# Interleaved first matmul groups, context rounding and small loads moved, and a new bank for the last half tile

## What is computed

```python
query = jnp.einsum('bnc,dc->bnd', teacher_features, Wq) + bq
key = jnp.einsum('bnc,dc->bnd', teacher_features, Wk) + bk
energy = jnp.einsum('bnd,bmd->bnm', query, key)
attention = jax.nn.softmax(energy, axis=-1)
x_m = jnp.einsum('bln,bmn->blm', teacher_logits, attention)
...
x = x + jnp.tanh(g_xattn[0]) * _L0_xattn_ref(_layernorm(x, axis=-1), ctx_1024, L0_xattn_Wq, L0_xattn_bq, L0_xattn_Wk, L0_xattn_bk)
x = x + jnp.tanh(g_ffn[0]) * _L0_ffn_ref(_layernorm(x, axis=-1), L0_ffn_weight, L0_ffn_gamma, L0_ffn_beta, L0_ffn_ln_weight, L0_ffn_ln_bias)
```

## Time and profile before

| | us |
|---|---|
| median of three runs | 124.51 |
| lowest, highest | 123.63, 124.8 |
| the profiled execution's own time | 123.77 |
| its span, first to last instruction | 121.9 |

### The profile page before, as it was taken

How to read it: one execution, slowest core, us unless ns; L and a number is a source line. 1 busy time by engine, 2 the same in 40 slices (tenths; PEclk the granted TensorE clock), 3 DMA queues, 4 the chain that set the end, 5 groups by cost and what they waited for, 6 DMA issues and landing times.

```text
span 121.9 us, 1882 instructions
## 1 busy us (share of the span) xinstructions
PE 116.8 (96%) x564; PEld 94.7 (78%) x564; DVE 94.8 (78%) x188; ACT 87.3 (72%) x186; POOL 93.0 (76%) x106
## 2 busy tenths in 40 slices
PE   5989999999999999999999999999999999999990
PEld 4658788888887988878888888888898888888870
DVE  1169599897898996769956993799749948989972
ACT  2455999999999979476998795659987962246200
POOL 3007999918247998999995999994748999999960
PEclk9999999999999999999999999999999999999998
DMA  4988999915813220027671302557000012220045
GB/s 92 273 291 286 404 386 321 345 52 163 239 41 132 95 77 5 3 86 255 261 258 25 147 5 86 167 177 232 27 3 3 0 74 103 86 86 0 0 168 176
DMA packets 10649, 17.15 MB, mean 141 GB/s; under 512 B 1808, under 2 KB 2576, under 8 KB 10640
## 3 DMA queue, kind: packets, MB, share of 16 engines
q1 hardware_dynamic: 9504, 16.78, 40.5%
q10 hardware_dynamic: 1136, 0.27, 1.0%
HBM read 12.59 MB, written 4.19 MB: 138 GB/s over the span
## 4 chain that ended last, share of the span: by engine, by line
PE 88%; DVE 6%; issue 2%; ACT 1%; DVEq 0%; ACTq 0%
PE ps_y L390 37%; PE ps_ffn L403 18%; PE ps_score L350 8%; PE ps_turn L357 5%; PE ps_score L357 3%; PE ps_score L464 3%; PE ps_y L357 3%; PE ps_y L320 2%; PE ps_turn L320 2%; PE ps_ffn L320 2%; DVE zt_lo L734 2%; PE ps_ffn L329 1%; PE ps_turn L350 1%; PE ps_ffn L456 1%; DVE ps_ffn L811 1%
## 5 line engine op out<-in xcount | busy, mean ns | idle before, releaser
L896 POOL TENSOR_TENSOR xt_lo<-xt_raw,xt_hi 128x512 fp32r<-128x512 f32 x16 | 21.1, 1319 | 5.8 <-ACT xt_hi L535 2.9
L390 PE MATMUL ps_y<-pt_hi,xt_hi 128*128 128x512 f32 x64 | 18.1, 404 | 0.0
L390 PE MATMUL ps_y<-pt_hi,xt_lo 128*128 128x512 f32 x64 | 17.5, 395 | 0.0
L390 PE MATMUL ps_y<-pt_lo,xt_hi 128*128 128x512 f32 x64 | 17.5, 395 | 0.0
L403 PE MATMUL ps_ffn<-w_sign,zt_hi 128*128 128x512 f32 x60 | 17.2, 408 | 0.0
L403 PE MATMUL ps_ffn<-w_sign,zt_lo 128*128 128x512 f32 x60 | 16.5, 396 | 0.0
L523 ACT ACTIVATE prob<-ps_score,neg_max 128x512 f32<-128x512 f32 x14 | 9.6, 687 | 9.5 <-DVE neg_max L676 9.5
L390 PEld LDWEIGHTS ps_y<-pt_lo,xt_hi 128*128 128x128 f32 x64 | 12.0, 188 | 3.0
L390 PEld LDWEIGHTS ps_y<-pt_hi,xt_lo 128*128 128x128 f32 x64 | 12.0, 188 | 2.9
L403 PEld LDWEIGHTS ps_ffn<-w_sign,zt_lo 128*128 128x128 f32 x60 | 11.3, 188 | 2.8
L748 DVE SCALAR_TENSOR_TENSOR ffn<-ps_ffn,rstd,gain 128x512 f32<-128x512 f32 x14 | 10.4, 743 | 3.8 <-PE ps_ffn L403 2.0
(11 more groups left out here) (178 smaller groups left out, 273.9 us busy)
## 6 DMA issues: line engine op xcount, KB each, us to landing
xt_raw<-in_x_t_dram SPq DMA_DIRECT2D x16, 256.0 KB, 3.0
ctx_sb<-in_ctx_t_dram SPq DMA_DIRECT2D x8, 256.0 KB, 5.5
x_sb<-in_x_dram SPq DMA_DIRECT2D x8, 256.0 KB, 5.3
ctx_sb<-in_x_dram SPq DMA_DIRECT2D x8, 256.0 KB, 6.4
out_dram<-x SPq DMA_DIRECT2D x8, 256.0 KB, 2.0
out_dram<-ctx_sb SPq DMA_DIRECT2D x7, 256.0 KB, 2.0
w_raw<-in_weight_t_dram SPq DMA_DIRECT2D x4, 256.0 KB, 7.5
ln_w<-in_ln_weight_dram SPq DMA_DIRECT2D x1, 256.0 KB, 7.5
```

What stands on the lines that cost most here:

```text
L390: mm = pe.matmul(ps_y[t % 2][:, :], lhs[:, t, k, :], rhs[:, k, :], start=(k == 0 and i == 0), stop=(k == KN - 1 and i == 2))
L896: nc.gpsimd.tensor_tensor(xt_lo[:, t, :, :], xt_raw[:, t, :, :], xt_hi[:, t, :, :].bitcast(f32), ALU.subtract).then_inc(xt_lo_done, 1)
```

## The change

Six edits.

1. The first two score tiles are computed together, term by term: both hi·hi, then both q_hi·k_lo, then both q_lo·k_hi (`first_scores`). Each term waits for its own operands; before, the first matmul waited for all of them (`proj_lo` at 2).
2. Batch 1's q and k projections are computed together, term by term (`first_projections`), the term that needs `ctx_lo` last.
3. Context 1 is rounded by POOL in place of DVE.
4. ACT rounds context 2 before `exps(0, 0)` in place of after it.
5. The three small loads (two gates, bias column) are issued by SP, behind the loads of x and ahead of those of the transposed x, in place of by ACT.
6. The last tile's first half goes to `ps_y[0]` in place of `ps_ffn[0]`, and PE waits for `x1_done` (the bank's last reader) in place of for tile 1's add. On DVE `finish` is split in `scale_in_place` and `add_scaled`, and tile 1's add goes behind `turned_ffn_lo(b, 3)`, which makes tile 3's lo part.

```diff
-        half_bank = (ps_ffn[T % 2], ps_score[0])
+        half_bank = (ps_y[0], ps_score[0])
...
             for t in range(T):
                 load_x(0, t)
+            sp.dma_start(gates[:, 0:1], g_xattn.rearrange("(a n) -> a n", a=1).broadcast_to([P, 1]))\
+              .then_inc(gates_in, 16)
+            sp.dma_start(gates[:, 1:2], g_ffn.rearrange("(a n) -> a n", a=1).broadcast_to([P, 1]))\
+              .then_inc(gates_in, 16)
+            sp.dma_start(lnb_col[:, :], ln_bias_t[:, :]).then_inc(gates_in, 16)
             for t in range(T):
                 load_xt(0, t)
...
+            def first_scores():
+
+                for n, (lhs, rhs) in enumerate(((q_hi, k_hi), (q_hi, k_lo), (q_lo, k_hi))):
+                    pe.wait_ge((proj_hi, proj_lo, proj_lo)[n], (2, 1, 2)[n])
+                    for t in range(HALF):
+                        mm = pe.matmul(score_bank(0, t)[:, :], lhs[:, 0, t * P:(t + 1) * P], rhs[:, 0, :],
+                                       start=(n == 0), stop=(n == 2))
+                        if n == 2:
+                            mm.then_inc(score_ready, 1)
+
+            def first_projections():
+
+                pe.wait_ge(w_lo_done, 2)
+                pe.wait_ge(ctx_hi_done[0], 1)
+                for n in range(3):
+                    if n == 2:
+                        pe.wait_ge(ctx_lo_done, 1)
+                    for j, (w_hi, w_lo) in enumerate(((wq_hi, wq_lo), (wk_hi, wk_lo))):
+                        for k in range(KC):
+                            mm = pe.matmul(proj_bank[1][j][:, :], (w_hi, w_lo, w_hi)[n][:, k, :],
+                                           (ctx_hi, ctx_hi, ctx_lo)[n][:, 0, k, :],
+                                           start=(n == 0 and k == 0), stop=(n == 2 and k == KC - 1))
+                        if n == 2:
+                            mm.then_inc(proj_ready, 1)
...
-                pe.wait_ge(last_out_done, 1)
+                pe.wait_ge(x1_done, T * b + 3)
...
-            for t in range(T):
+            first_scores()
+            for t in range(HALF, T):
                 scores(0, t)
-            project(1, 0)
-            project(1, 1)
+            first_projections()
...
-            act.dma_start(gates[:, 0:1], g_xattn.rearrange("(a n) -> a n", a=1).broadcast_to([P, 1]))\
-               .then_inc(gates_in, 16)
-            act.dma_start(gates[:, 1:2], g_ffn.rearrange("(a n) -> a n", a=1).broadcast_to([P, 1]))\
-               .then_inc(gates_in, 16)
-            act.dma_start(lnb_col[:, :], ln_bias_t[:, :]).then_inc(gates_in, 16)
...
+            round_ctx(2)
             exps(0, 0)
-            round_ctx(2)
...
-                dve.wait_ge(last_scaled, (0, 1, 0, 2)[t] + (cols.start > 0))
+
+            def add_scaled(b, t, bank, cols):
+                dve.wait_ge(x1b_done, T * b + t + 1)
...
-                dve.wait_ge(x1b_done, T * b + 2)
-                finish(b, 1, ps_ffn[0], slice(0, N))
+                scale_in_place(b, 1, ps_ffn[0], slice(0, N))
                 turned_ffn_lo(b, 3)
+                dve.wait_ge(last_scaled, 1)
+                add_scaled(b, 1, ps_ffn[0], slice(0, N))
...
-            round_ctx(1)
...
+            for k in range(KC):
+                pool.wait_ge(ctx_in[1][k], 16)
+            nc.gpsimd.tensor_copy(ctx_hi[:, 0, :, :], ctx_sb[:, 1, :, :]).then_inc(ctx_hi_done[0], 1)
             rest_ctx(1)
```

More of the change, by code:

```diff
@@ L689, in rest_qk @@
                          .then_inc(proj_lo, 1)
-            def round_ctx(b):
-                for k in range(KC):
-                    dve.wait_ge(ctx_in[b][k], 16)
-                nc.vector.tensor_copy(ctx_hi[:, b - 1, :, :], ctx_sb[:, b, :, :]).then_inc(ctx_hi_done[b - 1], 1)
             def stats_x(b, tiles):
```

7 lines of the change are left out of this document (4 added, 3 removed).

## The result

| | median | range | profiled execution | its span |
|---|---|---|---|---|
| before (18 runs) | 124.37 us | 123.62 to 125.06 | 123.77 | 121.9 |
| after (18 runs) | 125.18 us | 124.5 to 125.72 | 125.02 | 123.2 |

The ratio is 1.0061 (95% interval 1.004 to 1.0083): 0.6% slower, some 0.8 us, within the one per cent either way but above the predicted range of 122.9 to 124.8. I had forecast 123.8.

The account below looks back on a forecast made before the run. PE alone was taken to bound 21.90 to 110.01 us, PE and ACT together the opening. From 123.77, +0.05 (opening) and -0.40 (end) gave 123.4; half the difference to the runs' median raised it to 123.8, range 122.9 to 124.8.

Parts of the forecast that it names:

- the seam: Start of `attend(0, 0)`, where PE's and ACT's chains were said to arrive within 0.06 us, the later one deciding.
- the same set of transfers ends when it ended before: Opening loads: small loads queued behind x on SP would finish at the old 14.73 us, delaying ACT's tanh by 0.1 us.
- second rival: Opening: small loads land late, ACT stands at the tanh; 124.6 us for landing at 15.6, 126.0 at 16.95; chance 0.12.
- Cost nothing, gain nothing: Opening: casting context 1 on POOL causes no stall, and DVE's first maximum 0.5 us earlier is of no use to ACT.
- In that stretch the change alters nothing: From 21.90 to 110.01 us PE alone bounds the kernel; an earlier or later start shifts its end by the same time.
- The last store stays the last: Kernel's end: SP's first-half store is issued before 119.41, so the last store, moved from 119.81 to 119.41, remains last.
- The rival that the end gains nothing: Kernel's end: DVE's add before tile 2's scaling, or a store by SP, sets the end; 124.2 us, chance 0.1.
- The opening: Up to `attend(0, 0)`: PE 0.64 us earlier, ACT -0.02 or +0.1 later; the later chain decides, entered as +0.05 us.
- slower by over one per cent: Whole kernel: outcome more than 1% slower, tied to a small-load landing after 16.3 us; chance 0.06.

Follow-up runs that it names:

- the loads back: The changed kernel with the three small loads issued by ACT's queue again, all else as changed; ratio 1.0017 to the kernel before.
- the first kernel with the store on ACT's queue: Changed kernel without interleaving, tanh moved later, three spare DVE instructions early, last tile's first-half store moved from SP to ACT; ratio to before 0.9886 over five executions.

## Why the prediction was wrong, step by step

The prediction named two signs of being wrong, `attend(0, 0)` after 22.1 and new gaps of PE behind it. Both came: it started at 22.45, and PE stood 0.21 us at 47.28.

- **Edit 1: right.** 0.64 us forecast, 0.68 measured, worth 0.5 us once ACT is not in the way.
- **Edit 2: right on q, in part by luck on the total.** I forecast that ACT takes q at 13.45, 0.02 us earlier than before, with the head starts of PE and ACT eaten, a cost of some 0.9 us. In the changed kernel ACT took q at 13.26, 13.40 if the quicker first projection (-0.14) is taken off; with the loads back at 13.62, 13.38 less the slower one (+0.24). Kernels with edits 1 and 4 that differ by the interleaving alone are 0.9 to 1.0 us apart. In the traces 0.4 of that came in batch 0, where I had nothing, and hangs on the pause of edit 3; the seam alone lost 0.5.
- **Edit 5: the failed step that cost most.** "The last small load lands at about 14.73 us, and ACT's tanh starts at 14.8": it landed at 15.65, and ACT waited 1.06 us in place of 0.1. The step that failed is "the same set of transfers ends when it ended before": x's last tile landed 1.1 us earlier than before, at 13.61, but the last small load 2.0 us behind it, and the first load of the transposed x at 16.21 in place of 15.42. I took the old landing of x's last tile for that of the loads behind it. The rows, in which the three small loads share one semaphore, so that 5.5, 5.8 and 7.1 are its first, second and third filling:

```profile
x_sb<-in_x_dram SPq DMA_DIRECT2D x2, 256.0 KB, 6.5
...
gates<-in_g_xattn_dram SPq DMA_DIRECT2D x1, 0.5 KB, 5.5
gates<-in_g_ffn_dram SPq DMA_DIRECT2D x1, 0.5 KB, 5.8
lnb_col<-in_ln_bias_t_dram SPq DMA_DIRECT2D x1, 2.0 KB, 7.1
```

  The row that would have told it was in the profile of before and I did not use it. The same three loads, on ACT's queue:

```profile
gates<-in_g_xattn_dram ACTq DMA_DIRECT2D x1, 0.5 KB, 5.7
gates<-in_g_ffn_dram ACTq DMA_DIRECT2D x1, 0.5 KB, 7.1
lnb_col<-in_ln_bias_t_dram ACTq DMA_DIRECT2D x1, 2.0 KB, 7.6
```

  They took as long there. Issue at 8.59 plus 7.6 is 16.2, a wait of 1.5 us, at the late end of the 14.5 to 16.4 that the traces show. My second rival, late loads, had the mechanism and at its own 15.6 gave 124.6; I gave it 0.12. The rule of the Trainium skill on rings (DMA: Bandwidth & Descriptors, Queues, rings and completion order), which I set against this edit, would have a small load on SP stand in line behind SP's backlog. The late landing agrees, but `lnb_col` landed 2 us behind x's last tile and took 7.6 us on the other ring, so a place in line is not the whole of its time.
- **Edit 4: right as a need, its worth under-told.** The rounding left the solid stretch; I gave it nothing, since q came late anyway. Without the interleaving it is worth 0.5 us. It waits for its data, 1.07 us until 9.70, and holds up the first exponential, which starts at 10.67 though its row maximum was there at 10.00; before, it started at 10.51. ACT still had 0.49 us to spare ahead of q.
- **Edit 3: "Cost nothing, gain nothing" failed twice.** The cast took 1.04 us on POOL from 8.43, as priced, and `ctx_lo` was in time. It keeps a wait of 0.47 us away from PE when the interleaving is off, and moving it off DVE brought the pause of 0.34 us.
- **"In that stretch the change alters nothing" failed.** 0.54 us were lost behind 21.90. PE was one row after another there before, which doesn't tell how little time DVE had to spare; its pause of a third of a microsecond makes 0.42 of the 0.54 us, and 0.12 come with the interleaving.
- **Edit 6: right on PE, wrong for the time.** 0.40 forecast, 0.38 measured on PE. "The last store stays the last" was right too; that it would take as long beside its neighbour as alone was the silent assumption. Some 0.3 us went there. The rival that the end gains nothing (0.1) named a store by SP that would set the end. ACT's store stayed the last, but SP's beside it made it slower.
- **Sum.** For the profiled execution I had 123.4, and it is 125.02. The opening is 0.8 above its term, batch 0 0.5, the end 0.3, which is the whole difference; all three had the same sign. The forecast itself, 123.8, was 0.7 under the median of three runs before (124.51), of which the sum gave 0.35 and the rest came from leaning half on one quick execution. From the median of 18, 124.37, the sum alone would have been 124.0, against 125.18. A slip in the chances: slower by over one per cent would have needed a landing after some 16.6, not 16.3. Nor was every large load issued long before 8 us, as I wrote: SP issued the transposed x from 8.30 to 10.87. Neither changes the sum.

## What to carry to other kernels

Price a moved transfer by its own row of issue to landing, from the new issue, as a range and not as one time, and only then ask what else could hold it; and put an instruction that waits for a small late load behind work that doesn't need it. Interleaving two sums by term makes the first result late by the other's share (four matmuls, 0.94 us here), so it pays only if the wait that it shortens is longer than that. A last store brought closer to its neighbour took 0.3 us longer here, so read a gain on the last engine down to the landing of the last store.

## What the hardware showed unexpectedly

- **The first projection's pace.** The four fp32 matmuls of the first key projection took 1.94 us before, 1.88 in the changed kernel, and 3.26 with the loads alone on SP; the difference, up to 1.3 us, shifts all that follows. They run at 0.43 us each or at 0.85, and change over at another point in each execution. It isn't the edits: the kernel with edit 6 alone has the opening of before, and its four take 1.08 us longer. The windows show a granted clock of 1.00 in either case, so what the records call granted doesn't tell it. It is large enough for most of the scatter of one kernel's times (1.4 us before), though no kernel has two usable profiles to show that, and it is why every table above begins behind it. The rows, before and with the loads alone on SP:

```profile
4.59 1.94 PE L329 MATMUL ps_ffn<-ctx_sb,wk_sb 128*128 128x512 f32 x4
```

```profile
4.58 3.26 PE L334 MATMUL ps_ffn<-ctx_sb,wk_sb 128*128 128x512 f32 x4
```

- **One execution at half pace throughout.** One execution of the first kernel with the store on ACT's queue took 237.98 us, its other five 122.51 to 123.35. In its profile all matmuls ran at half pace (a stream of `attend` 0.45 us from start to start, where the same kernel run again has 0.24) with the granted clock shown as 1.00, and the other engines' durations were as ever. Windows (from:to, length, busy us of PE, PEld, DVE, ACT, POOL, clock, DMA share, GB/s):

```profile
50.00:120.00 70.00, 70.00 (x172) 45.66 (x171) 28.30 (x63) 29.91 (x67) 27.85 (x31) 1.00 0.19 60
```

- **The small loads' traffic.** From 8.00 to 11.00 the changed kernel moved 404 GB/s, from 11.00 to 14.00 179, where the earlier trace rows have 206 and 406. The slow stretch is not the time since their issue (7.62 to 8.59 in the changed kernel) but that in which their packets move: of packets under 512 bytes there are 67 in the first window and 431 in the second, and 357 and 117 before. The slow stretch moved with these packets.

```profile
8.00:11.00 3.00, 3.00 (x15) 2.39 (x14) 2.61 (x6) 1.77 (x3) 2.48 (x2) 1.00 1.05 404
11.00:14.00 3.00, 3.00 (x15) 2.40 (x14) 1.84 (x7) 2.51 (x8) 3.00 (x2) 1.00 0.54 179
```
